# Scatters paced by head steps, and the stage between two expert feed-forwards in a new order

## What is computed

```
x = x + attention(layernorm(x))    # 16 heads of 16, 4 key/value groups, rotary, causal, 50*tanh(s/50)
x = x + ffn(layernorm(x))
x = x + recurrence(layernorm(x))
x = x + ffn(layernorm(x))          # the same weights again
```

```
r, i = sigmoid(x @ Wa.T + ba), sigmoid(x @ Wx.T + bx)
a = exp(-8 * softplus(-Lam) * r);  u = sqrt(1 - a**2) * (i * x);  h_t = a_t * h_(t-1) + u_t
scores = softmax(x @ gate.T)               # 64 experts in 8 groups: best 3 groups, then best 6 experts
slot   = expert * 96 + min(position among the expert's tokens, 95)
y      = sum of 6 of  Wd @ (silu(Wg @ buf) * (Wu @ buf)), weighted by score   # inner width 176
out    = y + Sd @ (silu(Sg @ x) * (Su @ x))                                  # shared expert, width 352
```

## Time and profile before

| | |
|---|---|
| median of 3 runs | 1483.82 us (1474.37 to 1488.47) |
| the profiled execution | 1465.4 us, its span 1463.6 us |
| mean granted TensorE clock | 0.857 of full speed |
| TensorE matmul busy | 1058.7 us, 72% of the span |
| ScalarE busy | 709.3 us, 48% |
| VectorE busy | 519.1 us, 35% |
| GpSimd busy | 386.9 us, 26% |
| 192 scatters to the experts' buffer | 187.2 us, mean 0.975 us |

### The profile page before, as it was taken

The page is one execution under the profiler, slowest core; times in us unless marked ns, Lnnn a source line. Parts: engine busy times, 40 slices in busy tenths (PEclk is TensorE's granted clock), DMA queues, the critical chain, the costliest instruction groups (busy, mean ns, idle before and its releaser), DMA issues.

```text
span 1463.6 us, 18870 instructions
## 1 busy us (share of the span) xinstructions
PE 1058.7 (72%) x6648; PEld 627.3 (43%) x6648; DVE 519.1 (35%) x1557; ACT 709.3 (48%) x921; POOL 386.9 (26%) x336
## 2 busy tenths in 40 slices
PE   5868777876877587575559988467777534799874
PEld 3533233322322132123359977344444312698762
DVE  7752421551213122103323322146454432133226
ACT  2368989895999599493024433023020200244330
POOL 3000000024000600600535644103241516365450
PEclk9889889898999889787879999689786757799995
DMA  9970000002000200004847998811310232489977
GB/s 355 393 277 0 1 1 1 15 32 78 1 1 15 88 15 1 19 0 113 243 86 175 288 254 209 243 60 55 141 70 30 83 96 63 92 200 285 257 184 290
DMA packets 94925, 176.11 MB, mean 120 GB/s; under 512 B 13118, under 2 KB 46879, under 8 KB 94832
## 3 DMA queue, kind: packets, MB, share of 16 engines
q1 hardware_dynamic: 71216, 146.48, 31.9%
q0 software_dynamic: 23616, 28.44, 9.4%
HBM read 107.30 MB, written 83.72 MB: 131 GB/s over the span
## 4 chain that ended last, share of the span: by engine, by line
PE 22%; DMA 8%; issue 8%; DVE 5%; another core or an unknown queue 4%; SPq 3%; DVEq 1%; ACT 1%; POOL 0%; POOLq 0%; ACTq 0%
PE PS L1303 9%; DMA WD_space<-in_wd 6%; PE PS L1314 5%; PE PS L1375 2%; SPq L1082 2%; PE PS L1241 1%; PE PS L1290 1%; PE PS L1341 1%; SPq L1083 1%; DMA spare_space<-expert_out 1%; PE PS L1228 1%; DMA XE<-expert_in 1%; DMA expert_out<-ob,yidx 0%; POOL expert_out L1193 0%
## 5 line engine op out<-in xcount | busy, mean ns | idle before, releaser
L293 POOL DMA_INDIRECT expert_in<-xp,didx x192 | 187.2, 975 | 771.5 <-DVE didx L280 586.0
L659 ACT ACTIVATE PR<-PS 128x1024 f32<-128x1024 f32 (+3 forms) x320 | 275.0, 930 | 109.4 <-remote 38.3
L664 ACT ACTIVATE PR<-PR 128x2048 f32<-128x2048 f32 (+3 forms) x160 | 271.5, 1699 | 0.0
L567 PE MATMUL PS<-PR,V 128*32 128x512 f32 (+3 forms) x1280 | 171.5, 597 | 88.4 <-ACT PR L664 84.4
L1193 POOL DMA_INDIRECT expert_out<-ob,yidx x128 | 180.7, 1411 | 182.0 <-ACT ob L1475 137.5
L555 PE MATMUL PS<-QT,KT 96*128 96x512 bf16 (+3 forms) x640 | 181.6, 378 | 52.9 <-ACT PR L659 42.1
L1303 PE MATMUL PS<-XT,WGU 128*88 128x96 f32 x1600 | 152.6, 249 | 18.9 <-DMA WD_space<-in_wd 18.1
L1303 PEld LDWEIGHTS PS<-XT,WGU 128*88 128x88 f32 x1600 | 147.6, 159 | 36.9 <-DMA WD_space<-in_wd 25.6
L555 PEld LDWEIGHTS PS<-QT,KT 96*128 96x128 bf16 x640 | 59.1, 104 | 166.3 <-ACT PR L659 114.9
L1657 DVE SCALAR_TENSOR_TENSOR gta<-gth,PS 88x192 f32<-88x192 f32 x128 | 44.8, 350 | 222.5 <-ACT gth L1465 183.9
L1465 ACT ACTIVATE gth<-PS 88x192 f32<-88x192 f32 x128 | 41.9, 328 | 132.6 <-PE PS L1303 131.4
(11 more groups left out here) (245 smaller groups left out, 1350.8 us busy)
## 6 DMA issues: line engine op xcount, KB each, us to landing
WGU<-in_wgu SPq DMA_DIRECT2D x100, 352.0 KB
WD_space<-in_wd SPq DMA_DIRECT2D x100, 176.0 KB
expert_out<-zero SPq DMA_DIRECT2D x2, 8256.0 KB, 50.4
expert_in<-zero SPq DMA_DIRECT2D x2, 7776.0 KB, 39.3
XE<-expert_in SPq DMA_DIRECT2D x32, 486.0 KB
spare_space<-expert_out SPq DMA_DIRECT2D x24, 512.0 KB, 5.3
spare_space<-in_wgu SPq DMA_DIRECT2D x20, 352.0 KB
normed<-xp SPq DMA_DIRECT2D x8, 512.0 KB, 2.9
```

The costliest lines, as they stand in the source:

```text
L293: pool.indirect_dma_start(out=buf_d[f], out_offset=bass.IndirectOffsetOnAxis(ap=didx[b][:, r, j:j + 1], axis=0), in_=xp[b][:, r, :], in_of ...
L567: last = pe.matmul(PS[VW * j:VW * (j + 1), AV0 + unit % 2, cols(c, s):CW], V[:, g, s, :], PR[:, n % 3, j, cols(c, s):CW], start=(s == 0), ...
L659: act.activation(PR[:, n % 3, 2 * pr:2 * pr + 2, cols(c, s):CW], PS[:, S0 + 2 * pr:S0 + 2 * pr + 2, cols(c, s):CW], ACT.Tanh, scale=1.0 / ...
L664: act.activation(PR[:, n % 3, :, lo:CW], PR[:, n % 3, :, lo:CW], ACT.Exp, scale=SOFT_CAP).then_inc(exp_done, 1)
```

## The change

Two things change.

In attention, `dispatch_rows` takes a pace. The POOL program waits on `exp_done` ahead of each of the 72 scatters: the first chunk's follow head steps 28 and on of chunk 2 with one scatter a step, the second's steps 22 and on of chunk 3 with one a step, the third's steps 47 and on with two a step.

```diff
-                for k in range(K0):
-                    dispatch_rows(pool, k)
+                dispatch_rows(pool, 0, (first_step(2, 0) + 28, 1))
+                dispatch_rows(pool, 1, (first_step(3, 0) + 22, 1))
+                dispatch_rows(pool, 2, (first_step(3, 0) + 47, 2))
...
             for r in range(CT):
                 for j in range(TOPK):
+                    if paced:
+                        pool.wait_ge(exp_done, paced[0] + (r * TOPK + j) // paced[1])
                     pool.indirect_dma_start(
```

```diff
             for c in range(NC + 1):
                 k = NC + c - 1
-                if c < NC:
-                    combine(0, c)
                 if c:
                     turn_rows(k)
+                if c < NC:
+                    turn_recur(c)
+                if c:
                     logits(k)
-                    shared_in(k, 0)
                 if c < NC:
                     gates(c)
                 if c:
                     place(k)
-                    shared_in(k, 1)
-                    shared_in(k, 2)
+                if c >= 2:
+                    shared_down(k - 1)
+                if c + 1 < NC:
+                    for half in range(2):
+                        overflow_rows(c + 1, half)
+                if c:
                     turn_over(k)
                 if c < NC:
                     turn_state(c)
                 if c:
-                    shared_down(k)
+                    for j in range(SC):
+                        shared_in(k, j)
+            shared_down(NC + K0)
             experts(1)
```

```diff
+            def statistics(c):
+                if c:
+                    dve.wait_ge(xr_ready, c)
+                if c >= 2:
+                    dve.wait_ge(rows_ready, NC + c - 1)
+                dve.drain()
+                row_statistics(dve, c if c < NC else None, c - 1 if c else None).then_inc(stats_ready, 1)
+
+            def add_results(c):
+                for r in range(CT):
+                    dve.wait_ge(y_ld[r], 16 * (c + 1))
+                    tables = GB[:, r, :].rearrange("p (j q n) -> p j q n", j=NACC // 2, q=2)
+                    dve.tensor_tensor(tables[:, :, 0, :], tables[:, :, 0, :], tables[:, :, 1, :], ALU.add)
+                dve.drain()
+                dve.tensor_tensor(GB[:, :, 0:C], GB[:, :, 0:C], GB[:, :, 2 * C:3 * C], ALU.add)
+                dve.drain()
+                xc = X[:, CT * c:CT * (c + 1), :]
+                dve.tensor_tensor(xc, xc, GB[:, :, 0:C], ALU.add).then_inc(results_free, 1)
...
             for c in range(NC + 1):
                 k = NC + c - 1
-                if c:
-                    norm_rows(k)
-                if c < NC:
-                    combine(0, c)
-                    recur_rows(c)
+                statistics(c)
+                if c >= 2:
+                    for j in range(SC):
+                        shared(k - 1, j)
+                    last_tokens(k - 1)
+                if c + 1 < NC:
+                    add_results(c + 1)
                 if c:
                     shift(k)
-                    shared(k, 0)
                     choose(k)
                 if c < NC:
                     recur_inputs(c)
                 if c:
+                    slots(k)
                     destinations(k)
-                    shared(k, 1)
                 if c < NC:
                     recur_states(c)
-                if c:
-                    shared(k, 2)
-                    last_tokens(k)
+                if c + 1 < NC:
+                    add_overflow(c + 1)
+                if c >= 2:
+                    shared_add(k - 1)
                 if c < NC:
                     recur_add(c)
-                if c:
-                    shared_add(k)
+            for j in range(SC):
+                shared(NC + K0, j)
+            last_tokens(NC + K0)
+            shared_add(NC + K0)
             experts(1)
```

More of the change, by code:

```diff
@@ L1149, in _ @@
             results(0, 0)
+            results(0, 1)
             for q in range(EU):
                 weights(E + EX + q)
-            for c in range(1, NC):
-                results(0, c)
             for c in range(NC - 1):
+                if c + 2 < NC:
+                    results(0, c + 2)
                 store_normed(sp, NC + c)
@@ L1485, in experts, with normalize, turned_recur @@
                 out(E - 1)
-            def gates(c):
+            def normalize(c):
+                k = NC + c - 1
+                act.wait_ge(stats_ready, c + 1)
+                if c:
+                    b = k % NXP
+                    act.wait_ge(dispatched[b], 16 * CT * TOPK * (k // NXP))
+                    act.wait_ge(stored[b], 16 * (k // NXP))
+                    if k - NXP >= K0:
+                        act.wait_ge(rowsT_psum, k - NXP - K0 + 1)
+                    for r in range(CT):
+                        last = act.activation(xp[b][:, r, 0:C], X[:, CT * (c - 1) + r, :], ACT.Identity,
+                                              scale=rstd[:, CT + r:CT + r + 1], bias=shift_by[:, CT + r:CT + r + 1])
+                    last.then_inc(rows_ready, 1)
+                if c < NC:
+                    if c:
+                        act.wait_ge(xrT_psum, c)
+                    for r in range(CT):
+                        last = act.activation(xr[:, r, :], X[:, CT * c + r, :], ACT.Identity, scale=rstd[:, r:r + 1], bias=shift_by[:, r:r + 1])
+                    last.then_inc(xr_ready, 1)
+            def turned_recur(c):
                 act.wait_ge(xrT_psum, c + 1)
@@ L1498, in gates, with decays @@
                                    bias=lam[:, 4 + j // 2, j % 2:j % 2 + 1]).then_inc(gates_tanh, 1)
+            def decays(c):
                 act.wait_ge(gates_tanh, 4 * c + 4)
+                if c:
+                    act.wait_ge(x3_ready, c)
+                for h in range(CH):
+                    act.activation(qa_[:, h, :], ra_[:, h, :], ACT.Exp, scale=lam[:, 7, h:h + 1], bias=lam[:, 7, h:h + 1])
                 for h in range(CH):
@@ L1617, in destinations @@
                 slot_values(dve, k)
+            def destinations(k):
+                n = k - K0
                 if n:
```

206 lines of the change are left out of this document (107 added, 99 removed).

## The result

The changed kernel takes **1391.4 us** (median of 4 runs, 1385.9 to 1392.3) against 1479.1 us for the kernel before, run on the same chip (4 runs, 1474.0 to 1488.5): ratio 0.939, 95% interval 0.933 to 0.945. 1385 was forecast, -99 us; it became -88 by the medians and -79.5 by the two profiled executions (1465.4 and 1385.9). Part of the closeness of 1391.4 to 1385 is luck: the forecast was counted from a median of 1483.8, and the kernel before came out at 1479.1.

The account below looks back on a forecast made before the run. Bound: ScalarE in attention except where scatter bursts hold TensorE back, and a chain through all engines in the middle. -52 + 2 - 49 = -99 us on a median of 1483.8 gave 1385 us, range 1362 to 1438.

Parts of the forecast that it names:

- Scatters in attention, -52: Attention: pacing the scatters by head steps removes the slow steps beside dense bursts, -52 us (bounds -53 and -34).
- Rival 3: Attention: bursts innocent, or scatters cost the same wherever they stand, so nothing returns there; about 1436 us, chance 0.10.
- the Trainium skill's rule: Attention: DMA never contends with a compute engine, TensorE and ScalarE never wait on anyone; the scatter term would be 0.
- Between the stages, +2: Between attention and experts: two shared input projections ahead of the placing matmuls start the fourth burst later, +2 us.
- Up to the first burst, -9: Middle stage: the first burst starts at 999 instead of 1008.1, -9 us.
- chunk 0 saves 3 us: Middle, before the first burst: VectorE additions replace TensorE's identity passes, saving chunk 0 3 us up to x3.
- From burst to burst, 56, 56 and 54: Middle: times between burst starts fall from 67.6, 71.4 and 66.9 us to 56, 56 and 54.
- the pair of rows in the prediction: Middle: the same 16 gate passes took 9.32 us after an idle stretch against 7.13, suggesting a slower TensorE clock.
- the 2 us a step: Middle: allowance per step for TensorE's slower clock after passes are taken from it, 2 us.
- Rival 2: Middle: VectorE, not TensorE, stands still in a burst, so steps take 62 to 65 us; about 1409 us, chance 0.18.
- After the last burst, 40.0: Middle's end: 40.0 us from the last burst's start to the experts stay, added passes hidden under the burst.
- the dense burst: Attention and middle: scatters back to back slow TensorE, 0.88 us a pass by the middle's rows; spaced scatters do not.

Follow-up runs that it names:

- e1: Kernel before with only attention's scatters paced by head steps, old middle stage kept: 1421.3 us, ratio 0.962.
- e6: Changed kernel with attention's scatters in groups of eight back to back, at the same mean rate: 1400.6 us.
- e10: Changed kernel with attention's scatters in groups of twelve back to back, at the same mean rate: 1412.5 us.
- e9: Kernel before with attention's scatters paced and those of chunks 4 to 6 in three groups of eight, old middle stage kept: 1385.5 us, ratio 0.944.
- e3: Changed kernel with the indices of chunks 4 to 6 pointing past the table, so their 72 scatters are issued but move no rows: 1379.8 us.
- e5: Changed kernel with one scatter for each of chunks 4 to 6, then 30 drained GpSimd subtractions in place of the other 23: 1339.7 us.
- e4: Changed kernel with one scatter instead of 24 for each of chunks 4 to 6: 1333.5 us.
- e11: Changed kernel with the scatters of chunks 4 to 6 in four groups of six: 1337.0 us, ratio 0.912.
- e8: Changed kernel with the scatters of chunks 4 to 6 in three groups of eight: 1349.4 us, ratio 0.912.
- e7: Changed kernel with each scatter of chunks 4 to 6 waiting until the one before has landed: 1456.0 us, ratio 0.988.
- e12: Kernel before with attention's scatters paced and one scatter instead of 24 for each of chunks 4 to 6, old middle stage kept: 1355.2 us.

## Why the prediction came out right, point by point

- **Scatters in attention, -52.** Right, in size and place: -52.4 in the trace, 53.5 us when done alone (e1). Taken from the slow steps' excess over 3.61 us. Rival 3 is refuted by e1. The slow steps' start 14 us into a burst already said that the first scatters are free; e6 and e10 made it six or seven. That the Trainium skill's rule (0 for this term) was set aside for the rows was right here.
- **Between the stages, +2.** From the last long exponential to the experts' first transpose it is 697.20 - 610.29 = 86.9 us, before 745.73 - 662.66 = 83.1: +3.8.
- **Up to the first burst, -9.** Mis-sized: -2.9. From x3 to D the sum held: 956.69 - 924.80 = 31.9 for 30.3 to 32.5. What failed is "chunk 0 saves 3 us": the addition that makes x3 starts 53.9 us after the last scatter, 50.5 before, and 48 by the forecast. The overflow product, which I hadn't priced, now goes in two halves through one PSUM bank, each behind VectorE's addition of the half before, and TensorE's eight transposes back of the state (L1399) stand behind the second half, so that 5.1 us lie between the end of the scan and x3 (918.50 to 923.58), 2.1 before:

```profile
919.57 2.07 PE L1351 MATMUL PS<-O,WovT 64*128 64x256 f32 x4 [9.93 <-DVE X L1759]
921.57 1.97 PE L1399 MATMUL PS<-consts,spare_space 128*128 128x128 f32 x8
```

  The 50.5 is itself a low reading: in e1 and e9, with the same old middle, x3 starts 53.0 and 52.9 us after the last scatter and D4 comes at 92.3 and 92.1 instead of 89.8. Against these two the new middle saves 5 us up to the first burst.

- **From burst to burst, 56, 56 and 54.** Mis-sized: 60.8, 61.1 and 56.6, -27.4 in place of -39.9. The step was right up to where TensorE is released. The text left open whether passes end slowly inside the burst (a release as from D+28.5) or only after it (D+35.5), and 56 us with 22.3 behind the release stand for D+33.7; the third tanh stands at D+35.0, D+34.9 and D+34.9, so the second is what happens, and 1.3 us of a step's 4.8 are missed there. The other 3.5 are in the sum behind it, where 22.3 us were added up and 25.8 measured (991.70 to 1017.52): the two normalisations take 2.06 and 2.07 us instead of 3.2 together, the recurrence's transposes (1.94) stand before the logits, and the gates take 8.69 us at a granted clock of 0.81 instead of 7.13 at 1.00. TensorE's clock in the stage is 0.68 granted, against 0.75 before, in the direction of the pair of rows in the prediction and of the Trainium skill's rule that it cites; the 2 us a step allowed for it were of the right size. 35.0 + 25.8 = 60.8.
- **Rival 2**, steps of 62 to 65 because VectorE stands still, gave 1409; steps of 61 are nearer to it than to the forecast. Its cause is there in part: VectorE's small instructions are late in a burst as well (9.9 us of statistics for 3.5). But they are done 11 us before the third tanh; the chain waits for TensorE's passes, in e3 and in the changed kernel.
- **After the last burst, 40.0.** Right: 40.05. The passes of the last chunk ended late (VectorE has them at 1170.83, TensorE records their end at 1158.5), under the cover of the burst, as said.
- **That TensorE is slow in "the dense burst"** was right, but what in it makes TensorE slow was not said, and theory A of e3, that it is the moving of the rows, fell.

The gain was 19.5 us under the forecast by the profiled executions (11 by the medians): 12.5 us are the three steps, 6.1 the first burst, 1.8 the stretch between; attention (0.4) and the second experts (0.7) give 1 back. And the rewriting's reason was weaker than its gain: 21.6 of its 27.4 us between bursts are a shorter chain, the other 6 (9 by e1) work got out of a burst's way.

What stays open is the mechanism: what in 24 scatters back to back holds TensorE and VectorE from about the eighth on, when neither their rows (e3) nor GpSimd's being busy (e5) does, and pauses of 1 to 7 us after each six avoid it. The rows with idle time put down to "issue" say that instructions begin late; whether they reach the engines late, or are carried out or reported late, no run here tells apart. The Trainium skill, "DMA: Bandwidth & Descriptors", section "SWDGE vs HWDGE vs iDMA", says that GpSimd's software writes such descriptors into rings in SBUF, from which the DMA engines take them; no run here shows what a ring does to TensorE.

## What to carry to other kernels

Look at what runs on GpSimd beside an unexplained wait, even if no data of it is waited for: here 24 indirect DMAs in a row cost attention and each step of the middle 14 to 19 us (on all chips but one, see below), and the cheapest cure was a pause of a few us after every six, at events of the work beside them, without moving anything else. Pause by count, not by waiting for each to land: the landing wait stretched 24 of them from 31 to 79 us and became the chain itself. And take the burst away once (one scatter in place of 24) before rebuilding a stage to hide it: that one run tells how much hiding can bring.

## What the runs showed of the hardware that was not expected

- Scatters that drop all their rows hold TensorE as long as those that write them: third tanh at D+34.9 and D+35.0 (e3).
- The hold reaches VectorE: its small instructions, 0.17 us each, begin up to 1.4 us apart in the second half of a burst (statistics 9.9 and 9.1 us; 3.5 with one scatter, e4, and with groups of six or eight, e11 and e8).
- About six or seven scatters 1.28 us apart are free (an estimate from e6 and e10), each further one costs the engines beside it 0.9 to 1.0 us; at one every 3.3 us there is no hold over 79 us (e7), nor at two per 3.6 us.
- **One chip did not show the hold at all.** Beside e12 the kernel before was run once on that chip and took 1356.1 us, where 25 runs on other chips took 1460.5 to 1488.5; and e12, with paced scatters in attention and without three bursts, took 1355.2 us there. So on that chip bursts and no bursts differed by 0.9 us. It is one run of each, and no trace of the kernel before was taken there, but e12's own trace has two full bursts of 24, after attention (from 654.96) and after the middle (from 1108.17), scatters 1.28 us apart as elsewhere. In both VectorE adds the shared expert as soon as TensorE's passes are recorded as ended, after waits of 7.24 and 4.36 us; in e9, the same code there on another chip, it waits 20.62 and 18.34 us for "remote". VectorE's timelines, first burst, e12 and then e9:

```profile
677.15 1.22 DVE L1603 TENSOR_TENSOR X<-X,PS 128x1024 f32<-128x1024 f32 x1 [7.24 <-PE PS L1260]
```

```profile
688.60 1.22 DVE L1601 TENSOR_TENSOR X<-X,PS 128x1024 f32<-128x1024 f32 x1 [20.62 <-remote]
```

  So the pacing should be worth little on such a chip, and of this change some 20 us be left (an estimate from e4 and e12; the changed kernel never ran there). Whether it is the chip or how the program was placed on it isn't known. It also says what the holds cost the kernel before elsewhere, if nothing else differs: 113 to 123 us by the medians, of which 52 are in attention, 55 to 59 between the middle's bursts, and the rest is not placed.
